# Moving the split of the normed frames into the last slot's exponentials, and the copies of R ahead of Gelu's third part

## The reference

```python
h = tok(x)                          # frames -> DFT power -> mel -> log -> dct -> projection, 192 wide
h = h + attn(layernorm(h))
h = h + ffn(layernorm(h))

# attn, 8 heads of 64, values of 24
h1 = rmsnorm(x, norm1_w)
q, k, v = h1 @ wq, h1 @ wk, h1 @ wv
bias = (q.w_pos.basis + u.k + v.w_pos.basis) * scale
attn = softmax(q @ k.T * scale + bias)
x = (attn @ v) @ wo + bo + x
x = gelu(rmsnorm(x, norm2_w) @ w1 + b1) @ w2 + b2 + x

# ffn: each expert takes its 1000 best tokens; a shared expert takes all
```

## Time and profile before

| | us |
|---|---|
| median of 3 runs | 2087.18 (2084.29 to 2087.2) |
| profiled execution, its own time | 2081.72 |
| its span | 2080.1 |
| PE busy | 1912.6 (92%) |
| PE weight loads busy | 1634.6 (79%) |
| DVE busy | 1364.8 (66%) |
| ACT busy | 1070.9 (51%) |
| POOL busy | 704.5 (34%) |

### The profile page before, as it was taken

One profiled execution on the slowest core, in us unless ns is written; L12 is line 12 of the kernel. 1 busy time (PEld: TensorE's weight loads), 2 busy tenths in 40 slices (PEclk: granted clock), 3 DMA queues, 4 the chain that ended last, 5 costly groups with the idle time before them and its releaser, 6 DMA issues. The chain is left out here.

```text
span 2080.1 us, 46488 instructions
## 1 busy us (share of the span) xinstructions
PE 1912.6 (92%) x13428; PEld 1634.6 (79%) x13428; DVE 1364.8 (66%) x3748; ACT 1070.9 (51%) x2588; POOL 704.5 (34%) x587
## 2 busy tenths in 40 slices
PE   2899999999999999999958899799999999999997
PEld 2688888888888888888847787688888888888886
DVE  2577878878878878878746777455555555555531
ACT  2687787887887887887732221222222222222221
POOL 0122222222222222212210002266666665566663
PEclk9999999999999999999979999899999999999999
DMA  5666666666766666666636333244454554444451
GB/s 154 167 164 174 186 172 173 188 170 172 191 168 172 193 166 175 188 167 178 189 89 164 98 99 90 64 81 82 82 93 83 99 99 83 79 78 81 81 95 19
DMA packets 318048, 272.95 MB, mean 131 GB/s; under 512 B 80732, under 2 KB 305326, under 8 KB 317998
## 3 DMA queue, kind: packets, MB, share of 16 engines
q1 hardware_dynamic: 238878, 235.53, 42.1%
q0 software_dynamic: 70656, 30.65, 10.2%
q10 hardware_dynamic: 8464, 6.15, 0.9%
HBM read 151.25 MB, written 120.54 MB: 131 GB/s over the span
## 5 line engine op out<-in xcount | busy, mean ns | idle before, releaser
L1211 POOL DMA_INDIRECT out<-ff_y,ff_idxs x128 | 261.8, 2045 | 232.7 <-DVE ff_y L1490 175.0
L1266 ACT ACTIVATE ff_sg<-ffp_g 128x500 f32<-128x500 f32 x192 | 113.0, 589 | 384.5 <-PE ffp_g L1602 384.5
L1198 POOL DMA_INDIRECT ff_xg<-xs_d,ff_idxg x128 | 206.3, 1612 | 284.4 <-issue 269.4
L524 ACT ACTIVATE sb_prob<-sb_ssb,sb_mx 125x250 f32<-125x250 f32 x512 | 253.3, 499 | 61.0 <-DVE sb_rinv L614 33.1
L1614 PE MATMUL ffp_d<-ff_wd,ff_wide 128*125 128x192 f32 x1536 | 261.2, 327 | 7.7 <-DVE ff_wide L1477 6.7
L1477 DVE TENSOR_TENSOR ff_wide<-ff_sg,ffp_u 128x500 f32<-128x500 f32 x192 | 129.4, 674 | 207.9 <-PE ffp_u L1602 207.9
L1602 PE MATMUL ffp_g<-ff_xsp,ff_wsp 128*128 128x500 f32 x960 | 250.8, 391 | 7.6 <-issue 6.0
L1614 PEld LDWEIGHTS ffp_d<-ff_wd,ff_wide 128*125 128x125 f32 x1536 | 247.8, 188 | 11.2 <-issue 9.1
L1602 PE MATMUL ffp_u<-ff_xsp,ff_wsp 128*128 128x500 f32 x960 | 250.1, 390 | 0.0
L1602 PEld LDWEIGHTS ffp_g<-ff_xsp,ff_wsp 128*128 128x128 f32 x960 | 180.1, 189 | 45.3 <-issue 9.5
L822 PE MATMUL ps_qps<-sb_hsp,sb_wsp 128*128 128x250 f32 x1280 | 184.5, 291 | 32.0 <-DVE sb_hsp L728 22.8
(11 more groups left out here) (190 smaller groups left out, 3528.0 us busy)
## 6 DMA issues: line engine op xcount, KB each, us to landing
bias_d<-sb_rsb SPq DMA_DIRECT2D x256, 219.6 KB
sb_bsk<-bias_d SPq DMA_DIRECT2D x256, 218.8 KB
hx_d<-sb_hx SPq DMA_DIRECT2D x32, 336.0 KB
sb_hxl<-hx_d SPq DMA_DIRECT2D x32, 336.0 KB
ff_wd<-WdT SPq DMA_DIRECT2D x16, 576.0 KB, 5.0
xs_d<-sb_xs SPq DMA_DIRECT2D x32, 238.0 KB
bias_d<-sb_rsb SPq DMA_DIRECT2D x256, 25.5 KB
sb_bsk<-bias_d SPq DMA_DIRECT2D x256, 25.4 KB
```

What stands on the lines that cost most here:

```text
L524: a.activation(prob[:, s % 2, t], ssb[:, s % 2, t], ACT.Exp, bias=mx[:, s % 2, t:t + 1], scale=-1.0, accum_out=rs[:, t, s:s + 1]).then_inc ...
L1198: g.indirect_dma_start(xg[:, t], None, xs_d[:, :], bass.IndirectOffsetOnAxis(idxg[:, t:t + 1], 0), bounds_check=last).then_inc(gat, 16)
L1211: g.indirect_dma_start(out_d[:, :], bass.IndirectOffsetOnAxis(idxs[:, t:t + 1], 0), y[:, t], None, bounds_check=last, compute_op=ALU.add). ...
```

## The change

Three moves, with no operation added or removed. On ACT, in slot 7, the two high parts of the normed frames go between the two exponentials. On DVE, in slot 7, the two low parts go behind the copy of the probabilities and ahead of the last stage's statistics. On ACT, Gelu's third part goes from the end of slot 5 behind slot 6's two copies of R, just ahead of the table load.

```diff
@@ scalar, slot loop
+                    if bc is not None and s == 6:
+                        act.wait_ge(c_mm, C_USES * bc + 4)
+                        a.activation(gT[:, 2], tps[:, 0:FRAMES], ACT.Gelu, bias=b1[:, 2:3]).then_inc(c_ev, 1)
                     if tables_stale:
                         a.preload_act_table_set(EXP_SET)
...
+                    def model_high():
+                        act.wait_ge(t_mm, T_USES * bt + 4)
+                        if bq is not None:
+                            act.wait_ge(q_mm, Q_USES * bq + QK_USE[-1] + 1)
+                        ps = bank2(tps, FRAMES, 128)
+                        for k in range(2):
+                            a.activation(hsp[:, 0, k], ps[:, k], ACT.Copy, scale=n1w[:, k:k + 1]).then_inc(t_hi, 1)
+
+                    if bb_ is None and bt is not None and s == 7:
+                        model_high()
...
+                            if t == 0 and bt is not None and s == 7:
+                                model_high()
...
-                        act.wait_ge(c_mm, C_USES * bc + 4)
-                        a.activation(gT[:, 2], tps[:, 0:FRAMES], ACT.Gelu, bias=b1[:, 2:3]).then_inc(c_ev, 1)
-                    if bt is not None and s == 7:
-                        act.wait_ge(t_mm, T_USES * bt + 4)
-                        if bq is not None:
-                            act.wait_ge(q_mm, Q_USES * bq + QK_USE[-1] + 1)
-                        ps = bank2(tps, FRAMES, 128)
-                        for k in range(2):
-                            a.activation(hsp[:, 0, k], ps[:, k], ACT.Copy, scale=n1w[:, k:k + 1]).then_inc(t_hi, 1)
@@ vector, slot loop
                     if s > 0:
                         pt_copy(bb_, s - 1)
+                    if bt is not None and s == 7:
+                        ps = bank2(tps, FRAMES, 128)
+                        dve.wait_ge(t_hi, 2 * (bt + 1))
+                        for k in range(2):
+                            ins = v.scalar_tensor_tensor(out=hsp[:, 1, k], in0=ps[:, k], scalar=n1w[:, k:k + 1], in1=hsp[:, 0, k].bitcast(F32),
+                                                         op0=ALU.mult, op1=ALU.subtract)
+                        ins.then_inc(t_ev, 1)
                     if bc is not None and s == 7:
                         b0 = D_CHAIN * bc
...
-                    if bt is not None and s == 7:
-                        ps = bank2(tps, FRAMES, 128)
-                        dve.wait_ge(t_hi, 2 * (bt + 1))
-                        for k in range(2):
-                            ins = v.scalar_tensor_tensor(out=hsp[:, 1, k], in0=ps[:, k], scalar=n1w[:, k:k + 1], in1=hsp[:, 0, k].bitcast(F32),
-                                                         op0=ALU.mult, op1=ALU.subtract)
-                        ins.then_inc(t_ev, 1)
```

## The result

The changed kernel takes 2105.27 us (median of 4 runs, 2098.8 to 2105.96), the kernel before 2085.73 in the same comparison (2082.9 to 2087.2): ratio 1.0088, 95% interval [1.0065, 1.0112], 19.5 us slower. The forecast was 2106.

What follows compares the result with a forecast made beforehand. The prediction took the loop PE, ACT, DVE, PE (31.34 us) to bound the round. 26 turns x 0.69 = 17.9, plus 1 for other crossings, made 19 us slower; on the median 2087.2 that gave 2106 us, range 2093 to 2112.

Steps and rivals of the forecast that it cites:

- The ring: The loop PE, ACT, DVE, PE from L809 to L809, 31.34 us, said to bound the round; PE's waits lie beside it.
- DVE's new sum: DVE's steps from slot 7's copy L587 to slot 0's L608: L608 at 410.02 instead of 409.33, 0.69 us later.
- the turn: DVE's sequencer between `d_v` and L608: loop add, branch, register operation and L608's waits, taken as 0.85 us from `d_v`'s start.
- The Trainium skill's rule: DVE's loop branch at about 108 ns: L608 0.43 us behind `d_v`, 7 us in all; the prediction went by the rows.
- High parts, Gelu's third part: On ACT: second exponential perhaps 0.1 us late, within PE's slack; Gelu's move brings `qk(3)` at best 0.28 sooner, worth nothing.
- The branch exposed in part: Rival at DVE's loop branch: L608 0.27 to 0.44 us late, 2095 to 2100 us; chance 0.12.
- no change: Rival at DVE's loop branch: sequencer runs far ahead, 0.2 us or less uncovered, 2084 to 2091 us; chance 0.08.
- the exponentials' slip: Rival on ACT in slot 6: slip outruns ACT's 0.40 us wait, adding up to 10 us, 2116 us; chance 0.04.
- Faster: Rival at L809: it does not wait for DVE's copy, so PE gains 16 to 24 us, 2063 to 2071; chance 0.06.

Runs made afterwards that it cites:

- The filler behind `d_v`: The changed kernel with a DVE sum of two constant tiles that nobody reads behind `d_v` in slot 7: 2104.45 us, 1.0096.
- The copy put first, looped and unrolled: The changed kernel with `bn_aggr`, `d_v`, DVE's last copy, reciprocal and normed rows opening slot 0 ahead of its bias and extremum: 2092.11 us looped, 2081.05 unrolled.
- the sum in the kernel before: The kernel before with an extra DVE sum that nothing reads behind the low parts in slot 7: 2094.16 us, 1.0045.
- the looped version with `inv_b` first: The looped kernel with DVE's copy first, plus ACT's slot 1 copy of the row inverses ahead of queries and keys: 2076.94 us, 0.996.

## Why the prediction was right

The mechanism held, and its main size with it. The closeness of the time itself, 2105.27 against 2106, is partly luck, as said under the total.

- **The ring, and what PE's waits are worth.** Right. 19.7 us of PE's waiting for the low part were removed and the round grew. Gelu's move alone took half of the other wait away, some 4 us, and changed nothing. A wait before one input of a product is worth nothing while its other input arrives at the same moment.
- **DVE's new sum.** 0.69 us was predicted, 0.68 measured, step for step: low parts 0.65 behind the copy's start (predicted 0.65), then 0.78, 0.71, 0.28, and 0.84 where I took 0.85. The idle of 0.68 named issue and PE's wait of 1.25 before L815 were both as foreseen. `qk(0)` came 0.50 sooner behind slot 7's copy (2.11 against 2.61), not 0.6, since it now waits 0.24 for ACT's copy of R, which the prediction did not name. It costs nothing, because PE stands before L815 anyway.
- **Why the turn was exposed.** The filler behind `d_v` that costs nothing, and 0.22 instead of 0.84 without the loop, show that it is the turn and not DVE's work. The unrolled kernels also have constants in place of registers, so they don't tell the branch from the register work of the turn, and what fills the 0.3 us behind the branch no run shows. That the sequencer passes `d_v` only when its wait is met agrees with the loop's add standing at 415.1; the runs don't show it apart from other reasons.
- **The Trainium skill's rule.** The Trainium skill, "Advanced Engine Details and Errata", section Control Flow Timing, gives about 108 ns for a compare-and-branch. By the estimate made from it L614 would have come 0.43 us behind `d_v`, and the loss would have been 7 us. The trace disagrees with that sum: 0.84, and 0.62 of it gone with the loop. The branch's own record is 56 ns; the rest is the time around it.
- **High parts, Gelu's third part.** Nothing for either, as predicted. The second exponential was not even 0.1 late: PE takes it up 1.27 us behind the copy's start, 1.28 before. Gelu's move made `qk(3)` only 0.14 earlier than before in its own kernel, not 0.28.
- **The total.** 19 us were predicted; 26 turns of 0.68 make 17.7, and the medians differ by 19.5. The two profiles show where the rest lies. The changed kernel is 1.1 us late at the first L809 of the loop (161.20 against 160.12), 19.2 behind it (1025.47 against 1006.30), and 20.4 at the tower's last product (1106.99 against 1086.59). Up to the loop's end the profile thus bears out the forecast of 19; the last 1.2 us, in the rounds that drain the stages, it left out. The two spans differ by only 17.0, so in this pair the untouched second part was 3.4 us shorter. And the 2106 stands on a median of 2087.2 for the kernel before. In the comparison that median was 1.5 us lower and the loss 0.5 us larger than forecast, so the two partly cancel.
- **The rivals.** The branch exposed in part, no change, and the exponentials' slip are excluded by 0.84 us, by the interval, and by ACT's 0.18 of idle that was left in slot 7. Faster, if the copy were not what L809 waits for, is refuted by the 1.25 us for just that copy.

Four expectations of the experiments were wrong. The low parts alone lost 17 us more than the ring gives, 15 of them with the clock. The kernel before gained 15 us by unrolling instead of 3 to 8. The copy put first, looped and unrolled, missed its gain until ACT's `inv_b` followed. There I had named the ring through ACT only as a rival, and it was 0.6 us a round away. Two more ended just below their range: 8.8 us for the sum in the kernel before (9 to 12 expected), and 7.5 us gained by the looped version with `inv_b` first (8 to 12).

## What to carry to other kernels

Before moving work to shorten a wait, look up when the other inputs of the waiting instruction arrive; if that is within the same tenth of a microsecond, follow the one that is later to the engine that sets it. In a hardware loop, what runs last before the branch is also what hides the loop's turn: keep a long instruction there. Here a short one that waits for its predecessor left DVE idle for 0.68 us a turn, and the round grew by as much. When one edge of a ring is shortened, price the next one before building: here it took both moves to gain 7.5 us, and the first alone lost 8.

## What the hardware showed unexpectedly

**TensorE's clock behind long waits of PE.** With the low parts alone moved, PE stands 1.7 to 1.8 us before L809 in the looped rounds, and in 10 stretches the granted clock then falls to 0.50, its lower level, 1.2 GHz. Windows of that kernel around the wait shown above (columns as in the earlier trace rows, the granted clock is third from the end):

```profile
391.80:394.30 2.50, 0.77 (x12) 0.49 (x15) 1.84 (x8) 0.82 (x3) 1.30 (x2) 0.99 0.86 245
394.30:397.50 3.20, 3.20 (x25) 2.19 (x18) 1.57 (x6) 0.88 (x4) 1.89 (x3) 0.50 0.73 197
397.50:398.50 1.00, 1.00 (x10) 1.00 (x9) 0.25 (x1) 0.89 (x3) 0.53 (x1) 0.92 0.00 0
```

PE was busy 0.77 of 2.50 us; in the next 3.20 it is busy throughout at half the clock, and L809 takes 1.69 us instead of 1.05. In the changed kernel, where the same wait is 1.25 us, the looped rounds have no such stretch, nor have they in the kernel before. The ten rounds with such a stretch take 34.0 to 34.1 us instead of 32.5, which makes 15 of the 17 us that the ring leaves open. The four runs of this kernel agree: the longer the run (2128.07, 2132.64, 2135.23, 2161.47 us), the lower its mean granted clock (0.978, 0.975, 0.974, 0.961). What decides whether the clock falls these runs don't tell: 26 waits of the looped rounds are 1.73 to 1.79 us long, and only ten were followed by a fall.

**A loop's turn is not only its branch.** Unrolling made the kernel before 15 us faster (0.9926) though the turn was covered there but for 0.11 us a round.
